# Unmasked softmax units: scores made a second time with the keys on the partitions and the maxima subtracted in PSUM, in place of turning the exponentials

## The reference

```python
# cross attention (q and k after an RMS norm)
scores = jnp.einsum('bqhd,bkhd->bhqk', q, k) * scale
probs = jax.nn.softmax(scores, axis=-1)
img_x = jnp.einsum('bhqk,bkhd->bqhd', probs, v_img)
...
# attention with a memory
scores = jnp.einsum('bsqhd,bthd->bqhst', qh, kh) * scale
probs = jax.nn.softmax(scores, axis=-1)
a_dot = jnp.einsum('bqhst,bthd->bsqhd', probs, vh)
```

## Time and profile before

| | us |
|---|---|
| median of 3 runs | 1888.0 (1886.93 to 1888.16) |
| profiled execution | 1885.4 |
| its span, first to last instruction | 1883.6 |
| PE busy | 1360.4 (72%) |
| DVE busy | 1290.3 (69%) |
| ACT busy | 654.8 (35%) |
| POOL busy | 208.7 (11%) |
| mean granted clock of PE | 0.78 |

### The profile page before, as it was taken

How to read it: one execution, slowest core, us unless ns; L and a number is a source line. 1 busy time by engine, 2 the same in 40 slices (tenths; PEclk the granted TensorE clock), 3 DMA queues, 4 the chain that set the end, 5 groups by cost and what they waited for, 6 DMA issues and landing times.

```text
span 1883.6 us, 37522 instructions
## 1 busy us (share of the span) xinstructions
PE 1360.4 (72%) x14598; PEld 1031.4 (55%) x14598; DVE 1290.3 (69%) x2573; ACT 654.8 (35%) x1530; POOL 208.7 (11%) x401
## 2 busy tenths in 40 slices
PE   1786777687678767786877687778776556399980
PEld 0674566566555645574656456556655345266650
DVE  3877697779677877877787769677876566533332
ACT  2234423433342345233423433343344223133330
POOL 1000001000000000000001000100000255500006
PEclk9896788688859875886689788868876666699995
DMA  9900000000000000000000000000000322111114
GB/s 349 311 2 1 8 8 1 1 13 2 1 1 14 2 1 1 13 2 1 2 13 2 1 13 3 1 1 2 2 1 1 119 105 90 45 60 57 61 46 132
DMA packets 47741, 70.10 MB, mean 37 GB/s; under 512 B 4736, under 2 KB 42048, under 8 KB 46016
## 3 DMA queue, kind: packets, MB, share of 16 engines
q1 hardware_dynamic: 44480, 59.08, 9.3%
q0 software_dynamic: 3072, 8.39, 1.3%
HBM read 36.40 MB, written 31.06 MB: 36 GB/s over the span
## 4 chain that ended last, share of the span: by engine, by line
issue 65%; PE 16%; DVE 8%; POOL 6%; ACT 2%; SPq 1%; DMA 0%; POOLq 0%; DVEq 0%; ACTq 0%
PE ps L863 12%; POOL rstd L1298 3%; POOL experts L767 2%; SPq L818 1%; POOL rstd L1297 1%; PE ps L867 1%; DVE experts L639 1%; PE ps L455 1%; PE ps L382 1%; PE ps L965 1%; ACT big L1216 1%; DVE ptf L1465 1%; PE ps L428 1%; ACT experts L495 0%; DVE ptf L597 0%
## 5 line engine op out<-in xcount | busy, mean ns | idle before, releaser
L1216 ACT ACTIVATE big<-ps,st 128x128 f32<-128x128 f32 x768 | 205.5, 407 | 206.4 <-DVE st L1543 206.4
L965 PE MATMUL ps<-ident,big 128*128 128x128 f32 x1024 | 185.5, 349 | 33.9 <-ACT big L1216 18.3
L1465 DVE TENSOR_TENSOR ptf<-ps,ptf 128x1024 f16<-128x1024 f32 x128 | 154.6, 1221 | 67.2 <-ACT ptf L1222 65.9
L965 PEld LDWEIGHTS ps<-ident,big 128*128 128x128 f32 x1024 | 164.5, 186 | 60.7 <-ACT big L1216 31.6
L1222 ACT ACTIVATE ptf<-ps 128x1024 f16<-128x1024 f32 x128 | 130.6, 1030 | 91.7 <-PE ps L965 91.7
L1297 POOL TENSOR_TENSOR rstd<-mv,eps 128x1 f32<-128x1 f32 x80 | 18.3, 229 | 1278.2 <-DVE mv L1356 1278.2
L1541 DVE TENSOR_REDUCE st<-ps 128x8 f32<-128x1024 f32 x96 | 116.9, 1218 | 35.5 <-PE ps L863 35.5
L863 PE MATMUL ps<-wo,qhl 128*128 128x256 f32 x512 | 119.3, 388 | 15.1 <-DVE qhl L1470 12.6
L863 PEld LDWEIGHTS ps<-wo,qhl 128*128 128x128 f32 x512 | 96.0, 192 | 32.3 <-issue 13.2
L863 PE MATMUL ps<-experts,ptf 128*128 x468 | 108.7, 382 | 0.0
L867 PE MATMUL ps<-xT_h,wq_h 128*128 128x128 f16 x512 | 90.8, 222 | 0.0
(11 more groups left out here) (316 smaller groups left out, 3443.6 us busy)
## 6 DMA issues: line engine op xcount, KB each, us to landing
scratch<-mixT SPq DMA_DIRECT2D x10, 1920.0 KB, 16.7
big<-in_gu SPq DMA_DIRECT2D x8, 1024.0 KB, 5.1
ptf<-scratch SPq DMA_DIRECT2D x39, 128.0 KB, 2.0
scratch<-ptf SPq DMA_DIRECT2D x39, 128.0 KB, 1.7
kf<-in_dn SPq DMA_DIRECT2D x8, 512.0 KB, 6.0
xin<-in_x SPq DMA_DIRECT2D x16, 128.0 KB, 2.1
cin<-in_ctx SPq DMA_DIRECT2D x16, 128.0 KB, 2.6
big<-in_wq SPq DMA_DIRECT2D x2, 1024.0 KB, 6.3
```

The source lines that it names most:

```text
L965: m = pe.transpose(ps_f(u, j // 4, P, (j % 4) * P), big[u][:, j * P:(j + 1) * P], ident[:])
L1216: m = f(big[u][:, c], ps_all[u][:, c], ACT.Exp, scale=scale, bias=st32[u][:, 3, j:j + 1])
L1465: S(u, tt(pt_l[u][:, c], ps_all[u][:, c], pt_h[u][:, c], ALU.subtract), f"pt{n}l{h}")
```

## The change

For units 1, 3a and 3b the exponentials are no longer turned. Instead:

- DVE (`maxima`) writes the maxima of each head as a high and a low bf16 part to `peaks` (in `st32`), with a cast and a subtraction where one scaling stood.
- PE (`peaks_turned`, stages m10 to m3b1) turns them, two transposes of 128x8 for a half, into the PSUM bank of the half's first scores; ACT copies the eight rows to `peaksT` (in `wt`; `peaks_out`, mo10 to mo3b1), one copy of 8x256 for unit 1, two of 8x128 for the others.
- PE (`scores_turned`, d10 to d3b1) makes the scores of the half again with keys and queries exchanged, so that the keys are on the partitions, and behind each adds a product of eight rows, `less` (minus ones for the head's high and low row, a new constant of 128x4) with `peaksT`, which subtracts the maxima in PSUM.
- ACT (`exps`) takes two exponentials of 128x1024 from PSUM, one to f16 `pt_h` and one to f32 `big`; DVE's low part is `big` less `pt_h`.

The operands of unit 1 move to the second halves of `pt_l` and `pt_h`. Unit 0 keeps its transposes. All four tables are written anew, the first three with another place at which the loop closes. The core of the diff:

```diff
 TENSOR_TURN = """
-1:a61 1:kv1 0:T00 1:tr1 0:T01 1:a7 0:a50 0:a51 1:pkk 0:a52 0:a53 1:pk1 0:a60 1:c10 1:c11 0:a61 1:T10 1:T11
-0:kv1 1:pv1 1:pv1z 0:tr1 1:atr 1:prj 0:a7 0:pkk 1:tr2 1:a15 0:pk1 0:c10 1:a16 0:c11 1:a17 1:tr3 1:a19 0:T10
...
+1:pv1 0:pk1 1:pv1z 0:c10 1:atr 1:prj 0:c11 0:m10 0:d10 0:m11 1:tr2 1:a15 0:d11 1:a16 1:a17 0:pv1 0:pv1z 0:atr
...
 SCALAR_TURN = """
...
+0:qT3 1:mo3b1 1:e3b0 1:e3b1 0:mo3a0 0:mo3a1 0:e3a0 0:e3a1 1:a31s 1+a0s 0:mo3b0 0:mo3b1 0:e3b0 0:e3b1 1+v0h
...
+            less = sb_a("less", [P, 4], BF16)
+            peaks = [b[:, 3, 0:16].bitcast(BF16) for b in st32]
+            peaksT = [b[:].bitcast(BF16) for b in wt]
...
-            def p_transposes(u, n, h):
-
-                W(f"n0{h}" if n == "0" else f"e{n}{h}", u)
+            def p_transposes(u, h):
+
+                W(f"n0{h}", u)
...
+            def peaks_turned(u, n, half):
+
+                W(f"s{n}m{half}", u)
+                for b in (2 * half, 2 * half + 1):
+                    rows_, c = peak_at(n, b)
+                    m = pe.transpose(PS[u][rows_, 2 * half, :].bitcast(BF16)[:, c:c + P], peaks[u][:, 8 * b:8 * b + 8], identm[:])
+                m.then_inc(sig(f"mT{n}{half}", u), 1)
+
+            def scores_turned(u, n, half):
+
+                W(f"mo{n}{half}", u)
+                for j in range(8 * half, 8 * half + 8):
+                    q, k = operands(u, n, j)
+                    o = ps_f(u, j // 4, P, (j % 4) * P)
+                    rows_, c = peak_at(n, j // 4)
+                    mm(o, k, q, True, False)
+                    m = mm(o, less[rows_, j % 4:j % 4 + 1].to_broadcast([8, P]), peaksT[u][rows_, c:c + P], False, True)
+                m.then_inc(sig(f"d{n}{half}", u), 1)
...
-                else:
-                    for j in range(8 * h, 8 * h + 8):
-                        c = slice(j * P, (j + 1) * P)
-                        m = f(big[u][:, c], ps_all[u][:, c], ACT.Exp, scale=scale, bias=st32[u][:, 3, j:j + 1])
-                m.then_inc(sig(f"e{n}{h}", u), 1)
...
+            def exps(u, n, h):
+
+                W(f"d{n}{h}", u)
+                c = slice(1024 * h, 1024 * h + 1024)
+                scale = float(DHX if n == "1" else DHM) ** -0.5
+                f(pt_h[u][:, c], ps_all[u][:, c], ACT.Exp, scale=scale)
+                f(big[u][:, c], ps_all[u][:, c], ACT.Exp, scale=scale).then_inc(sig(f"e{n}{h}", u), 1)
+
+            def peaks_out(u, n, h):
+
+                W(f"mT{n}{h}", u)
+                for b in ((2 * h,) if n == "1" else (2 * h, 2 * h + 1)):
+                    rows_, w = (slice(64 * h, 64 * h + 8), 2 * P) if n == "1" else (slice(32 * b, 32 * b + 8), P)
+                    m = f(peaksT[u][rows_, 0:w], PS[u][rows_, 2 * h, :].bitcast(BF16)[:, 0:w], ACT.Copy)
+                m.then_inc(sig(f"mo{n}{h}", u), 1)
...
             def turned_low(u, n, h):
 
-                W(f"pt{n}h{h}", u)
+                W(f"pt0h{h}" if n == "0" else f"e{n}{h}", u)
                 c = slice(1024 * h, 1024 * h + 1024)
-                S(u, tt(pt_l[u][:, c], ps_all[u][:, c], pt_h[u][:, c], ALU.subtract), f"pt{n}l{h}")
+                S(u, tt(pt_l[u][:, c], (ps_all if n == "0" else big)[u][:, c], pt_h[u][:, c], ALU.subtract), f"pt{n}l{h}")
...
                 link(red(m_, p8, AX.X, ALU.max))
-                scale = float(DHX if n == "1" else DHM) ** -0.5
-                S(u, ts(st32[u][:, 3, 8 * h:8 * h + 8], m_, -scale, None, ALU.mult), f"s{n}m{h}")
+                high, low = [peaks[u].rearrange("p (b a i) -> p a b i", a=2, i=4)[:, a, 2 * h:2 * h + 2] for a in (0, 1)]
+                m2 = m_.rearrange("p (b i) -> p b i", i=4)
+                link(cp(high, m2))
+                S(u, tt(low, m2, high, ALU.subtract), f"s{n}m{h}")
```

More of the change, by code:

```diff
@@ L115 @@
+0+s01 0+n00 0+n01 1+a6v 0+l00 1+kvv 1+n1 0+l01 0+o0b 1+kvp 1+xT1 1+a7k 0+o0d 1+a7v 1+a8 1+a7q 0+a6v 1+s10
+1+s11 0+kvv 0+n1 0+kvp 0+xT1 0+a7k 0+a7v 1+l10 0+a8 0+a7q 1+l11 1+a11 1+a12 0+s10 1+a13 0+s11 1+n2 1+xT2
+1+a15v 1+a15t 0+l10 1+a16v 0+l11 1+a17v 0+a11 1+n3 1+xT3 0+a12 1+a19v 0+a13 1+a19e 0+n2 0+xT2
 """
@@ L839, in _ @@
             load(xn[0][:], A["mask"])
+            load(xn[1][:, 0:4], A["less"])
             load(rb[:], A["rb"].to_broadcast([P, E0]))
             load(memw[:, 0:1], A["memw"].to_broadcast([P, 1]))
-            assert len(consts) + 2 + 9 + 3 == n_consts
+            assert len(consts) + 2 + 9 + 4 == n_consts
             sp.wait_ge(sig("zeros"), 9)
@@ L1031, in keys1, with operands, peak_at @@
                 pack_transposes(u, 2, kp, 8).then_inc(sig("kT1p", u), 1)
+            def operands(u, n, j):
+                if n == "1":
+                    h = head_at(j, 2)
+                    r, c = slice(64 * (h % 2), 64 * (h % 2) + 64), slice((8 + h // 2) * P, (9 + h // 2) * P)
+                    return pt_h[u][r, c], pt_l[u][r, c]
+                hh = 16 * "ab".index(n[1]) + head_at(j, 4)
+                h, r = hh % NHM, slice(32 * (hh % 4), 32 * (hh % 4) + 32)
+                return qp[u][r, (hh // 4) * P:(hh // 4 + 1) * P], kp[u][r, (h // 4) * P:(h // 4 + 1) * P]
+            def peak_at(n, b):
+                return (slice(64 * (b // 2), 64 * (b // 2) + 8), b % 2 * P) if n == "1" else (slice(32 * b, 32 * b + 8), 0)
+            def peaks_turned(u, n, half):
[13 more added lines that the diff above has]
+                m.then_inc(sig(f"d{n}{half}", u), 1)
             def scores1(u, half):
@@ L1174, in _ @@
             f(mask[:], xn[0][:], ACT.Copy)
+            f(less[:], xn[1][:, 0:4], ACT.Copy)
             f(identb[:], ident[:], ACT.Copy).then_inc(sig("w_ready"), 1)
@@ L1234, in qkT @@
                 W(tr, u)
-                f((pt_h if nk == 8 else qp)[u][:, 0:1024], psb(u, 0), ACT.Copy).then_inc(sig(nm, u), 1)
+                f(pt_h[u][:, 1024:2048] if nk == 8 else qp[u][:, 0:1024], psb(u, 0), ACT.Copy).then_inc(sig(nm, u), 1)
             def a15(u):
@@ L1700, in shape_constants @@
         "decay": np.ascontiguousarray(dn.transpose(2, 0, 1)).astype(f),
+        "less": -np.tile(np.concatenate([np.eye(4), np.eye(4), np.zeros((24, 4))]), (4, 1)).astype(f),
         "iota8": np.broadcast_to(np.arange(NE, dtype=f), (P, NE)).copy(),
```

118 lines of the change are left out of this document (53 added, 65 removed).

## The result

The changed kernel takes **1965.65 us** (median of 4 runs, 1964.55 to 1967.16) against 1887.47 for the kernel before: a ratio of 1.0415, 95% interval 1.0397 to 1.0433. It is slower by 78 us, where 1866 us and a range of 1832 to 1914 were forecast; over eight turns that is 9.8 us a turn. The profiled execution took 1965.2 us.

A forecast was written before the change was run, and what follows sets the result against it. No single engine bounds it: PE and DVE are each busy 135 of a turn's 177.5 us, and engines wait in turn. Terms summed to -2.8 us a turn, times 8, +0.5 once: from 1888.0 to 1866 us, range 1832 to 1914.

The forecast's parts named there:

- Stretch B: Part of a turn from set 1's first maxima to set 0's mix, holding all twelve changed softmax halves; 104.2 us before.
- The switches: Changes of tile rows between unit 1's key and maxima products on PE: 0.10 us each, 64 a turn, 4.5 us on the path.
- DVE's edge: DVE's loop closing moves ahead of stage pk3v, where both sets wait for it: +1.5 us a turn (0 to 2.95).
- PE's edge: PE's loop closing moves ahead of unit 1's weighted sum: +0.4 us a turn, with DVE's as the bound.
- The placing: Stages of Stretch B placed by hand on the new tables at PE's low clock: end at 103.7 us against 104.2, -0.5.
- The bias: Hand placing of one old unit came out 4% long, so 4% was taken off Stretch B: -4 us a turn.
- Stretch A: Part of a turn from set 0's mix to set 1's first maxima, 73.3 us: two DVE stalls go, -3 and -1.7.
- The 0.5 us for one more load: Outside the turns, one more small constant on SP's queue: +0.5 us once.
- The chain: A unit 3 from its first maxima at the low clock: 10.6 us old and new, nothing won in the chain itself.
- (1): Rival: switches in unit 1 cost 0.15 us each, all 64 on the path; a turn +2.3, kernel 1907 us; 25%.
- (2): Rival: sets too close, each of 12 new trips costs 0.5 us more than placed; +3.2 a turn, 1914 us; 10%.
- signs of being wrong: Unit 1 half near 0.9 or over 3 us; low part off 1.22; B over 106; DVE idle over 7.1 or 1.5.

The follow-up runs named there:

- rows64: The changed kernel with a 64-row tile for unit 1's product that subtracts the maxima, so its changes of tile are gone: 1927.9 us.
- rows64_edge: rows64 with PE's loop closing ahead of unit 0's output projection, not ahead of unit 1's weighted sum: 1919.1 us.
- rows64_edges: rows64_edge with DVE's loop also moved, closing ahead of set 0's addition after unit 0, where DVE waits for PE anyway: 1906.8 us.
- after_edge: The changed kernel with only PE's loop edge moved, from ahead of unit 1's weighted sum to ahead of unit 0's output projection: 1959.9 us.
- before_dve: The kernel before with DVE's loop closing ahead of set 1's first maxima, not ahead of the low part of set 0's turned rows: 1880.7 us.
- neworder_edges: The kernel before (turned exponentials) under the changed kernel's four tables, with PE's and DVE's loop edges moved as in rows64_edges: 1888.3 us.
- neworder: The kernel before (turned exponentials) under the four tables of the changed kernel: 1905.2 us.
- pre4_pk3: rows64_edges with four key products a half ahead of the wait for ACT's copy, and PE's loop closing ahead of turning set 1's memory queries: 1878.1 us.
- fill4: rows64_edges with four useless f32 transposes a half placed in PE's idle during the wait for ACT's copy: 1921.7 us.

## Why the prediction was wrong

**Stretch B, term by term.** The forecast had B at 104.2 - 0.5 - 4 + 4.5 + 1.5 + 0.4 = 106.1 us; it took 116.1. The runs split the 10.0, in the order rows64, rows64_edge, rows64_edges:

- *The switches, 4.5:* B falls by 5.0 without them, and the kernel by 4.7 a turn. Right, as was the 0.10 us for each (0.16 from start to start, 0.05 to 0.07 in rows64). Error 0.5. (With PE's edge moved first, after_edge to rows64_edge, B falls by 6.2 and the error is 1.7.)
- *DVE's edge, 1.5:* 1.1 in B, 1.5 a turn on the kernel. Right, though it stood 2.57. Error -0.4.
- *PE's edge, 0.4:* 3.5 in B (2.3 if it is moved first). **This step failed**, by 3.1 (or 1.9). I took the price of an edge from the place where it stood. The rows of before couldn't show the price at pv1; the bound that I named (DVE's 2.95) would have been the safer value. It isn't the long products behind the old place that made it cheap, since ahead of the same products the new order stood 3.6 to 4.2 us; why it was 0.42 in the old order stays open. And of the 3.5 in B, 1.1 came back in A: on the whole kernel the move was worth 1.1 a turn.
- *The placing, 103.7:* without switches and with both edges elsewhere B is 106.5, 2.8 more. Of that 1.0 lies between 3a and the mix (57.2, placed 56.2), where I took 1.06 us for the 16 products of a unit 3 half by doubling a row of eight like products; as pairs they take 1.37, and grouping them gave 1.3 back. In groups they take 0.97, so the row was right for like products only. The other 1.8 lie ahead of 3a (49.3, placed 47.5), 0.8 of them ahead of the reciprocal; no run takes these apart.
- *The bias, -4:* **this step failed too**, by 4.0, and is the largest. Placing one old unit of 10.6 us came out 4% long (11.0), and I took 4% off a new stretch of 103.7; there the placing was 3% short (106.5). Everything was placed at the low clock, while B of the kernel before ran at 0.70 and the new one at 0.58; that this is the reason isn't shown (see the clock, below).

0.5 - 0.4 + 3.1 + 2.8 + 4.0 = 10.0.

**Stretch A, -4.7:** measured -1.0. The stall of 2.95 went, but DVE's edge alone is 1.3 of A (before_dve). The second low of unit 0 waited 0.9 in place of 1.7. What is late next took the rest. This term failed by 3.7 a turn, nearly as much as the bias. DVE's waits in A of the changed kernel, 806.58 to 878.43:

```profile
DVE xr L1514 <- PE ps L868: 4.2, 1, 4.2
DVE ptf L1504 <- ACT ptf L1265: 1.0, 2, 0.9
DVE st L1483 <- PE ps L872: 1.0, 1, 1.0
DVE big L1561 <- POOL rstd L1337: 0.9, 1, 0.9
```

DVE waits 4.2 us for the projection of set 0, where 3.8 stood ahead of the maxima, 1.0 for set 0's scores, where it had not waited, 0.9 for POOL in place of 0.4, and it has 0.7 us more work. I let the stalls go and didn't ask what comes behind each. The 0.5 us for one more load, the last term of the sum, stands on no row, and no run measures it.

**The clock.** In the same order with the same edges, B ran at 0.70 with turned exponentials (neworder_edges) and at 0.58 with second scores (rows64_edges). What the lower clock costs shows where one kernel has both: neworder in two turns, and pre4_pk3 in two.

```profile
673.09:779.84 106.75, 71.10 (x673) 52.87 (x671) 72.95 (x166) 46.94 (x131) 7.83 (x20) 0.70 0.01 1
851.13:960.67 109.54, 75.06 (x673) 55.40 (x671) 73.17 (x166) 46.93 (x131) 7.83 (x20) 0.64 0.01 1
```

```profile
660.57:762.09 101.52, 75.89 (x793) 52.76 (x791) 75.19 (x177) 38.35 (x67) 8.43 (x20) 0.63 0.01 2
835.34:938.95 103.61, 78.30 (x793) 54.48 (x791) 75.34 (x177) 38.35 (x67) 8.45 (x20) 0.59 0.01 2
```

The same instructions take 2.8 us more with the clock lower by 0.06, and 2.1 with 0.04. By that the fall from 0.70 to 0.58 would be worth some 6 us of B (an estimate, 0.12 at 2.8 for 0.06), which would cover the 4 of the bias. That the clock caused these differences, and was not caused by them, isn't shown: no run sets it alone, and fill4, which raised it without gain, added work too.

**The chain, "10.6 against 10.6":** it holds only while PE is free when the maxima are. In the new order 3b of set 1 takes 12.3 (placed 12.4), in the old one 14.0.

**The rivals.** (1) had the sign and a price that was too high; the switches were 38 of the 78 us. (2), the sets too close with 0.5 us a trip, is nearest in kind: the trip costs 3.4 us a turn, 0.29 for each of the 12, though that is the whole trip and not what was on top of the placing. Neither was made to carry an edge, and I gave no rival to it. The 35% for slower was too little for a change with four terms of unknown price.

**Small terms that held:** the low part (1222 ns, forecast 1221), the two activations (1026 and 1023 ns), a cast and a subtraction of 172 and 168 ns, a unit 1 half in 2.5 us at the full clock.

```profile
L1504 DVE TENSOR_TENSOR ptf<-big,ptf 128x1024 f16<-128x1024 f32 x96 | 116.6, 1222 | 54.2 <-ACT big L1252 53.2
L1251 ACT ACTIVATE ptf<-ps 128x1024 f16<-128x1024 f32 x96 | 98.5, 1026 | 44.2 <-PE ps L868 43.1
L1583 DVE CAST st<-st 128x8 bf16<-128x8 f32 x96 | 16.5, 172 | 3.3
```

Of the signs of being wrong that the prediction named, B over 106 and the idle ahead of pk3v (2.57, over 1.5) came up. So did the idle of DVE ahead of the low parts, over 7.1: in the turn shown it is 6.8 for units 1 and 3 and 1.0 for unit 0.

```profile
DVE ptf L1504 <- ACT big L1252: 6.8, 5, 2.4
```

It is no better than before in spite of an ACT that has 8.6 us less to do in B: the activations now start behind PE, as their row above shows (43.1 us of idle ended by PE). A unit 3 half (1.37, over 1.1) failed a sign of being right.

## What to carry to other kernels

Where a change moves the edge of an engine's loop, don't price it from the row at the old place: ahead of the same products it stood 0.42 us in one order and 3.6 to 4.2 in another. Give it a range, and put it where the engine waits anyway; rotating a table is a cheap experiment that leaves the order of the work alone. A correction for bias that comes from one unit of 10 us isn't to be taken off a stretch of 100, least of all one that may run at another clock. And work moved from one engine's parallel queue (ACT under PE) into a round trip must be placed against what stands in the other engine's queue at that moment.
